# A graph network kernel: scatters and gathers of GpSimd issued in shorter runs, each gated by another engine's count

## The reference

```
z   = [x[src], x[dst], edge] @ W.T + b          # 106250 x 256
z   = batch norm of z over all edges
msg = sigmoid(z[:, :128]) * softplus(z[:, 128:])
x1  = layernorm(x + (x + segment sum of msg by src))
mean = segment mean of x1[src] by dst
h   = x1 + 0.2 * mlp(x1) * tanh(norm(x1 - mean))
out = layernorm(x1 + (layernorm(h) * gamma + beta))
```

## Time and profile before

| | us |
|---|---|
| timed executions | 3959.84, 3949.55, 3946.03 |
| their median | 3949.55 |
| span of the profiled execution, first to last instruction | 5481.6 |
| busy in it: PE, DVE, ACT, POOL | 3436.3, 2979.6, 2242.8, 2626.3 |

### The profile page before, as it was taken

How to read it: one execution, slowest core, us unless ns; L and a number is a source line. 1 busy time by engine, 2 the same in 40 slices (tenths; PEclk the granted TensorE clock), 3 DMA queues, 4 the chain that set the end, 5 groups by cost and what they waited for, 6 DMA issues and landing times. The chain is left out here.

```text
span 5481.6 us, 84513 instructions
## 1 busy us (share of the span) xinstructions
PE 3436.3 (63%) x18854; PEld 2395.6 (44%) x18855; DVE 2979.6 (54%) x7781; ACT 2242.8 (41%) x6113; POOL 2626.3 (48%) x2634
## 2 busy tenths in 40 slices
PE   6745666666656888888888885661175555455542
PEld 2312222222223666666666664551165445445542
DVE  7975555555655333333333337971198555455547
ACT  1405555555654444444444448971197000000002
POOL 3775444444553555555555550077600544545542
PEclk8957777778877888888888887885587777777766
DMA  5322222122221666656666575463443221222213
GB/s 166 110 88 67 60 65 63 59 61 65 61 68 56 191 190 186 195 186 188 188 191 188 184 173 222 169 241 114 130 194 87 58 49 47 53 53 53 56 41 39
DMA packets 314711, 638.06 MB, mean 116 GB/s; under 512 B 54382, under 2 KB 188567, under 8 KB 306551
## 3 DMA queue, kind: packets, MB, share of 16 engines
q0 software_dynamic: 99440, 246.85, 16.9%
q1 hardware_dynamic: 172984, 266.76, 15.7%
q10 hardware_dynamic: 42192, 123.38, 6.1%
HBM read 424.53 MB, written 212.24 MB: 116 GB/s over the span
## 5 line engine op out<-in xcount | busy, mean ns | idle before, releaser
L367 POOL DMA_INDIRECT rec_d<-arena x830 | 887.8, 1070 | 815.8 <-issue 520.7
L853 POOL DMA_INDIRECT arena<-b_tab,arena x880 | 839.2, 954 | 730.4 <-DVE arena L874 405.8
L767 PE MATMUL psum<-arena 128*128 128x440 f16 x3360 | 776.5, 390 | 369.5 <-DVE arena L626 140.8
L626 DVE TENSOR_SCALAR arena<-iota_t,arena 128x880 f16<-128x880 f16 x840 | 516.1, 664 | 545.9 <-remote 320.5
L461 ACT ACTIVATE arena<-arena 128x128 f16<-128x128 f16 x1680 | 568.5, 388 | 469.9 <-remote 333.1
L767 PEld LDWEIGHTS psum<-arena 128*128 128x128 f16 x3360 | 344.2, 106 | 803.5 <-DVE arena L626 322.1
L1569 PE MATMUL psum<-arena,x_sb 128*128 128x129 f32 x2304 | 398.3, 347 | 454.2 <-DVE x_sb L1456 320.9
L964 PE MATMUL psum<-weT,arena 128*128 128x256 f32 x1760 | 627.6, 443 | 31.9 <-DVE arena L874 21.9
L1448 DVE TENSOR_TENSOR arena<-psum,arena 128x258 f32 x880 | 375.3, 426 | 476.9 <-remote 282.2
L1569 PEld LDWEIGHTS psum<-arena,x_sb 128*128 128x128 f32 x2304 | 375.7, 257 | 480.4 <-issue 192.3
L1255 POOL DMA_INDIRECT arena<-x_tab,arena x304 | 299.9, 987 | 556.1 <-DMA x_tab<-arena 295.9
(11 more groups left out here) (251 smaller groups left out, 5920.5 us busy)
## 6 DMA issues: line engine op xcount, KB each, us to landing
z_d<-arena ACTq DMA_DIRECT2D x220, 512.0 KB
arena<-z_d SPq DMA_DIRECT2D x44, 2560.0 KB
arena<-rec_d SPq DMA_DIRECT2D x220, 260.0 KB
arena<-in_edge_attr SPq DMA_DIRECT2D x83, 640.0 KB
arena<-early_d SPq DMA_DIRECT2D x34, 516.0 KB
arena<-b_tab,arena POOLq DMA_INDIRECT x880
rec_d<-arena POOLq DMA_INDIRECT x831
early_d<-arena POOLq DMA_DIRECT2D x9, 1032.0 KB
```

What stands on the lines that cost most here:

```text
L367: nc.gpsimd.indirect_dma_start(rec_rows, bass.IndirectOffsetOnAxis(e_idx[:, s, k:k + 1], 0), e_buf[:, s, k, :], None).then_inc(s_es[s], 16)
L626: nc.vector.tensor_scalar(hot_tile[:, s, :].rearrange("p (a b) -> p a b", b=TILE_RUN), iota_t[:, :, 0:TILE_RUN], tile_f[:, bass.ds(t, 1)], ...
L767: last = nc.tensor.matmul(bank(4 + 2 * k + h)[:, 0:HALF], hot_lane[:, s, k, :], hot_tile[:, s, h * HALF:(h + 1) * HALF], start=start, stop ...
L853: nc.gpsimd.indirect_dma_start(bg[:, s, k, :], None, b_tab, bass.IndirectOffsetOnAxis(rec[:, s, k, H:H + 1].bitcast(I32), 0)).then_inc(s_b ...
```

## The change

Three places on POOL's stream, nothing else. Line numbers behind L261 grow by 1, and by up to 16 at the end.

1. `scatter` takes a batch number. From group 21 on, the scatters of a group are issued as four, three and three: the fifth waits until ACT has made four columns of the batch beside it (`s_lane`), the eighth until it has made eight; in slot 2, which has two batches beside it, eight and sixteen.
2. The early gathers are issued in runs of four. Each run waits for `s_fl`, the first for 92, the last (67) for 218, evenly between.
3. `rows` and `gather` work by halves of a group, and each half has its own threshold of `s_sg`, except in the first four groups, which have none, as before. The eight direct groups at the end wait by halves as well.

```diff
+        BURSTS = {4: 4, 7: 8}
...
-                def scatter(it1, s):
+                def scatter(it1, s, batch=None):
                     pool.wait_ge(s_el[s], it1 * 16)
                     pool.wait_ge(s_er[s], it1 * 3)
                     settle(pool, s_turn)
                     for k in range(G_IN):
+                        if batch is not None and k in BURSTS:
+                            pool.wait_ge(s_lane, batch * G_IN + BURSTS[k] * (2 if s == IN_SLOTS - 1 else 1))
+                            settle(pool, s_turn)
                         nc.gpsimd.indirect_dma_start(rec_rows, bass.IndirectOffsetOnAxis(e_idx[:, s, k:k + 1], 0),
                                                      e_buf[:, s, k, :], None).then_inc(s_es[s], 16)
+
+                def scatter_beside_list(it, s):
+                    scatter(it + 1, s, 4 * it + (s - 4 * FILLED))
...
+        BURST, MESSAGES_FIRST = 4, EARLY_TILES // YG + 17
...
                     for k in range(G):
+                        if k % BURST == 0:
+                            pool.wait_ge(s_fl, MESSAGES_FIRST + (2 * g + k // BURST) * (CHUNKS * CG - MESSAGES_FIRST) // (2 * EARLY))
...
-                    if s < 2:
-                        wait(pool, s_sg, 24 * (2 * use) + (8 * s - 80))
-                    else:
-                        wait(pool, s_sg, 24 * (2 * use) + (8 * s - 72))
-                    settle(pool, s_turn)
-                    rows(s)
+                    for half in range(2):
+                        if not (isinstance(use, int) and use == 1):
+                            wait(pool, s_sg, 48 * use + (24 * (s // 2) + 12 * (s % 2) + 6 * half - 84))
+                            settle(pool, s_turn)
+                        rows(s, half)
...
-                    pool.wait_ge(s_sg, 8 * (3 * (before // 2) + 2 + before % 2 if before < 4 * ROUNDS else 2 * ROUNDS + before + 1))
-                    rows(n % XS)
+                    emptied = 8 * (3 * (before // 2) + 2 + before % 2 if before < 4 * ROUNDS else 2 * ROUNDS + before + 1)
+                    for half in range(2):
+                        pool.wait_ge(s_sg, emptied - 4 + 4 * half)
+                        rows(n % XS, half)
```

More of the change, by code:

```diff
@@ L372, in _ @@
                 pool.wait_ge(s_lza, 16 * len(LAST_BY_ACT))
-                with pool.Fori(0, N_GROUPS_IN // IN_SLOTS) as it:
+                with pool.Fori(0, FILLED) as it:
                     for s in range(IN_SLOTS):
                         scatter(it + 1, s)
+                for s in range(IN_SLOTS):
+                    scatter_beside_list(FILLED, s)
+                with pool.Fori(FILLED + 1, N_GROUPS_IN // IN_SLOTS) as it:
+                    for s in range(IN_SLOTS):
+                        scatter_beside_list(it, s)
                 for g in range(N_GROUPS_IN // IN_SLOTS * IN_SLOTS, N_GROUPS_IN):
-                    scatter(g // IN_SLOTS + 1, g % IN_SLOTS)
+                    scatter(g // IN_SLOTS + 1, g % IN_SLOTS, 4 * (N_GROUPS_IN // IN_SLOTS - FILLED) + g % IN_SLOTS)
                 pool.wait_ge(s_tl, 16)
@@ L1251, in _, with rows @@
                     pool.wait_ge(s_be[i], len(range(i, EARLY // 2, 2)) * 16)
-                def rows(s):
-                    for k in range(G):
+                def rows(s, half):
+                    for k in range(half * G // 2, (half + 1) * G // 2):
                         nc.gpsimd.indirect_dma_start(ring_slot(s)[:, k, :], None, x1_tab, bass.IndirectOffsetOnAxis(gi[:, s, k:k + 1], 0)).then_inc(s_xe[s], 16)
```

## The result

The change makes the kernel a little slower: 3962.55 us median of 5 runs (3955.02 to 3971.48) against 3946.03 (3937.52 to 3959.84) for the kernel before beside it, a ratio of 1.0048 with a 95% interval of 1.003 to 1.0066. The two medians are 16.5 us apart. The ratios and intervals here are not quotients of the medians; by the ratio the loss is 19 us, by its interval 12 to 26. Forecast were 3905 us and a gain. The measured time lies inside the range for 8 in 10 (3845 to 3982), but outside the forecast's own of 3870 to 3938, and the time moved the other way.

The account below looks back on a forecast made before the run. It took no engine to fill the list, messages or averages, which stalled during long runs of POOL's DMAs. Engines' need of 3824 us left 126 of the 3949.6 us median; 45 of these would go, giving 3905 (8 in 10: 3845 to 3982).

Parts of the forecast that it names:

- 126 us of stall: Whole kernel: the timed median of 3949.6 us less the 3824 us that engines need, taken as the most to be won.
- the late start: Messages: first early gather waits for 90 added segments instead of 80, 27.3 us later, said to cost nothing.
- The trace's own time against the timed one: Whole kernel: span 5481.6 us against median 3949.6; the trace's stalls called mostly an effect of tracing, at most 126 us winnable.
- sum of what engines need: Whole kernel: undisturbed paces of all stages added up, from 380 us of ranks to 86 of the end, 3824 us.
- The averages: Averages stage: 110 turns of 5.5 us, 605 us needed, where the first trace took 1146.
- A second sign: Averages: 608 direct gathers at 1.25 us would make 3979 us in all, so POOL must be faster in timed runs.
- What runs of four are worth: List, messages, averages: shorter runs of POOL's DMAs remove 65% of their stall; 45 us of the timed run.
- Scatters and halves: List scatters (124 added waits) and averages' ring by halves (76): waits at 0 to 0.30 us each, taken as 0.
- Early gathers: Messages: 272 gathers in 68 gated runs of four, starting 27.3 us later; free, with the end under 44 us of norm.
- The rival of the late gathers: Messages and norm: at 1.95 us per gather POOL is late already, so 27 us lost, 3977 us; chance 0.17.
- What would show it: Signs in the new trace: shorter list and message stalls, span about 4600 us, first direct gather right after x1's store.

## Why the prediction was wrong, step by step

Two steps failed. The gain of 45 us was a share of 126 us of stall that don't exist, and the late start, put at nothing, costs the 16.5 to 19 us that the change loses.

**The trace's own time against the timed one** is the first step that failed, and the others hang on it. The forecast saw that 1532 us of the profiled execution were in no timed run, and still took its terms from there. It called the stalls an effect of tracing; a second trace of the same program has none of them and a span of 3964.9 us, so tracing doesn't make them. And its sum of what engines need, 3824 us, had two large errors of opposite sign that nearly cancelled. Held against the second trace of before: ranks -18.5 (361.5 for 380), list +69.5 (841.5 for 772), edges -132 (1120 for 1252), norm +44 (88 for 44), averages +161 (766 for 605), end +15 (101 for 86), the rest about 0: together +140, which gives the 3964 us of the second trace's stages. The 1252 us were PE's busy time at a granted clock of 0.87, where an ordinary execution has 0.99 and 1057 us. The 605 of the averages and the 772 of the list left GpSimd out, which issues without a pause in both (766 and 841.5 us). So the 126 us that the forecast had to explain were no stall at all; with 132 too many in one place and 161 too few in another, the remainder could be given any meaning.

**The averages.** "A second sign" had the right number: 608 gathers at 1.25 us are 760 us, "155 more than the 605 of the turns", and the forecast then supposed that GpSimd's pace was better in the timed runs. It is not: 1.267 us after and 766 us of averages before. The row had said what bounds the stage, and was explained away since it didn't fit the sum.

**What runs of four are worth.** Forecast 45 us. The comparison of 0.32 us per gather in the edge stage with 0.93, 0.96 and 0.89 elsewhere set whole stages of one bad execution side by side. Measured: 0 for the gates beside the messages (1.0001, 0.9991 to 1.001), 0 for scatters and halves together (0.9998, 0.9987 to 1.0009). The step was wrong in its mechanism twice: there was no stall to shorten, and the gates made no shorter runs, since GpSimd, being late, found nearly all of them open.

**Scatters and halves** were costed at nothing for their waits, and that held, within 5 us for 200 waits. In the averages the gates are mostly open when GpSimd comes to them, and a gate is the gap that there is anyway: of GpSimd's waits at the direct gathers after the change, those put down to PE are

```profile
POOL x_sb L1270 <- PE psum L1585: 9.1, 30, 0.3
POOL arena L1270 <- PE psum L1585: 7.9, 26, 0.3
```

56 times, none longer than 0.3 us. The waits for ACT at the scatters in the list are the same (15.9 us, 52 times, at most 0.3).

**Early gathers.** This is the second step that failed, and the one that costs the time. "Now 90 must be, two chunks or 27.3 us later" was right (90 in the trace, 32 us later). "The late start costs nothing as long as POOL keeps up" failed in its condition: GpSimd is 80 us behind the last segment before the change, not inside the norm's 44. The cover that the step named was the right one, and it was already used up.

**The rival of the late gathers** was the mechanism, at a chance of 0.17. It was right that in undisturbed executions gathers beside the messages are slow (1.95 us each worked out, 1.75 and 1.66 measured) and that the first direct gather would then wait for early gathers. Its price of 27 us was too high, because it took each us of delay in full; 30.7 us cost 20, and the change's 32 us 16.5 to 19. The argument against it, that at 1.95 us "the list's and averages' POOL work would not fit in 3950", mixed two paces: beside DVE's work in the messages a gather takes longer, elsewhere the gathers are 1.26 us apart. Two near neighbours of the second trace of before show both, and below them stand two rows of VectorE beside the first:

```profile
2631.66 3.78 POOL L1245 DMA_INDIRECT arena<-x_tab,l_idx  x1 [0.30 <-issue]
2635.74 0.95 POOL L1245 DMA_INDIRECT arena<-x_tab,l_idx  x1 [0.30 <-issue]
```

```profile
2631.79 2.82 DVE L1380 SCALAR_TENSOR_TENSOR arena<-arena 128x2560 f32<-128x2560 f32 x1
2634.64 0.69 DVE L1387 TENSOR_TENSOR arena<-arena 128x512 f32<-128x512 f32 x1
```

The long gather ends at 2635.44, 0.83 us behind the end of L1380. VectorE makes no pause there; it goes on with L1387 at once.

That is also the place of the rule in the Trainium skill (SBUF — State Buffer, SBUF: two separate sides, its box on DVE and software DMA), that GpSimd can't write descriptors while DVE holds the shared port. The trace agrees with it, with 3.78 us against 0.95, and the run with the addition in pieces shows that it is VectorE's work that the gather waits for; that it is the port, no run here can show. The forecast drew the right result from it, a stage whose DVE is freed of stalls slows GpSimd, and then gave it too little weight.

**What would show it.** The text named the sign in advance: if the first direct gather "waits for early gathers instead, the late start is being paid". The rows of the norm above are that sign. The falls of the list's and messages' stalls, also named there as signs of being right, came true and mean nothing: the kernel before shows them as well in its second trace. The span fell to 3956.5 us and not to about 4600, further than any share of the change could explain. A sign counts only if the kernel before would not give it too.

## What to carry to other kernels

When a profiled execution is far longer than the timed ones (here 39%), no stage's length and no wait in it is a term for a sum (single instructions did hold: 0.95 us for an issue, 2.82 for L1380 in both traces); profile the same kernel again, and look first at a stage that the change doesn't touch. Add up the engine with the plainest pace, here one DMA issue each 1.26 us, over each stage before calling anything else the bound; if it comes out above the others, it is the bound. A gate on an engine that is already late does nothing: count in the trace how often a new wait is longer than the gap that was there before. A GpSimd that issues DMAs and is the bound can also pay for VectorE's long operations: look for a single issue of several us, and cut the operation beside it or move it. A delay of an engine that has slack in neither the stage it is in nor the ones behind costs the work that it would have done there times the price of that work later, here about 0.7 us per us. And when work is taken out of a stage, its price is that of the pieces that go, here the last ones, not the stage's mean.

## What the runs showed of the hardware

The same program with the same data once ran 5481.6 us under the profiler, with cross-engine waits of 10 to 43 us while GpSimd issued DMAs, and 3964.9 us the next time. Of fourteen profiled executions of this kernel and its variants this happened in the first only. What caused it is open.

A GpSimd gather can be held up by a VectorE operation with two inputs in SBUF. Of the 216 gathers beside the messages in the second trace of before, 71 take over 1.3 us, and each of the 71 ends 0.81 to 0.85 us behind the end of L1380 (27 of them) or of L1387 (44), which both combine two f32 tiles of SBUF. Not every gather beside them is held: the other 145 take 0.95 to 1.3 us. Over all 216 it is 100 us more than 0.95 each, and it comes from the 0.7 us operations as well as from those of 2.8. In the norm it is 9.36 us beside 9.1 us of addition and one-hots, and 2.81 beside 2.44 of one-hots alone. The 9.36 were removed by removing the addition, with 6.3 us of the time. That an addition of two f32 tiles, too, holds up software DMAs was not expected. The Trainium skill (SBUF — State Buffer, SBUF: two separate sides) lists an operation with two inputs in SBUF as one that takes the shared pair only against a GpSimd operation that reads SBUF, and its box on DVE and software DMA speaks of operations in a two-port mode. Here the gather beside the addition stood for the addition's whole length. The gather takes its row numbers from `l1_idx`, which lies in SBUF, so the first of the two may be what applies; no run here separates them.
